# Self-attention in a decoder layer: the projection bank is copied to an on-chip tile by ScalarE, and Pool splits v from the copy

## The chip, the cores and the metric

The kernel runs on one core of one Trainium2 chip. A core has a matrix engine (TensorE; PE in the profile, PEld for its weight loads), a vector engine (VectorE, DVE), a scalar engine (ScalarE, ACT), a general one (Pool, POOL) and SyncE (SP), which issues DMA transfers. Each engine works through its own list of instructions in order; they wait for one another by semaphores. TensorE writes its products to PSUM banks; the other tiles are on-chip (SBUF). The metric is the device time of one execution in microseconds.

## The reference, cut to what matters

A decoder layer: self-attention with rotary embedding on a layer-normed x, then a cross-attention block, then a mixture of experts. The change is in the first.

```python
q, k, v = (proj(Wq), proj(Wk), proj(Wv))            # [4 batches, 16 heads, 1024, 64], fp32
q = q * cos + rotate_half(q) * sin
k = k * cos + rotate_half(k) * sin
scores = jnp.einsum('bhqd,bhkd->bhqk', q, k) / math.sqrt(HD)
scores = jnp.where(causal, -jnp.inf, scores)
attn = jax.nn.softmax(scores, axis=-1)
out = jnp.einsum('bhqk,bhkd->bhqd', attn, v)
```

## The kernel before, in words

`self_attention` runs over 4 batches and, in each, over 8 pairs of heads (`j` counts pairs over all batches). fp32 accuracy comes from splitting each operand into a high part (a copy that rounds, name `_hi`) and the rest (a subtraction, name `_lo`); so a projection is three matmuls for each 128 rows of the contraction.

**Stages.** In each batch a `prologue` norms and transposes x (`xt_hi`, `xt_lo`), and projects pair 0. Then `attention(j)` computes pair j and at the same time projects pair j + 1: its 24 steps (one for each block of 128 keys of a unit; four units, a head and 512 queries each) are taken in 8 groups of 3, and each group projects one block `t` of 128 rows of the next pair into the bank `ps_qkv`: 128 columns each of q, k and v for two heads. TensorE's part of this, `qkv` (L336 to L350), is cut into 12, 6 and 6 matmuls at places 0, 1 and 2 of the group. The last pair of a batch projects nothing. The middle six attentions are a loop of three rounds with two pairs each; the branch back is taken twice in each batch.

**The order in a step** is written out by hand for each engine. TensorE: transposes of the probabilities (L431, which at a unit's first step wait until its rows are normalised), scores ahead (L371 to L375), the values' product of the step before (L415, L416), at place 1 the transposes of the rotated q and k (L359), then the projection part (L345). At place 0 this part waits for `qkv_read`, since there is one bank.

**The bank's readers.** After the last part, ScalarE copies v's high part (`split_v`, L479). VectorE then, in `rotate`, multiplies q and k by cos (L630, `r_cos`) and sin (L633, L634, `r_sin`), subtracts v's rest (L635), which signals `qkv_read`, and adds both products (L640, `rotated`). Then it takes the reciprocals of row sums (L663), for which ScalarE's `normalise` (L500) waits.

**The weights.** Pair j + 2's weights come in 8 blocks of 128x384 through 4 slots, `w_raw`: block k uses slot k % 4. ScalarE makes `w_hi` (L470): blocks 0 and 1 at step 22 of attention j, 2 and 3 at step 23, 4 and 5 at step 0 of attention j + 1, 6 and 7 at step 1. Pool makes `w_lo` (L274) in `rest_of_w`. SyncE loads block k + 4 (L231) once `w_lo` of block k is done. TensorE waits for `w_lo` of each block at the first of its three matmuls in block t = 0 of the next projection. At steps 0 and 1 ScalarE's exponentials (L492) come behind its weight blocks in its list.

**Pool's list** in a pair: w_lo 4 to 7, the store of the pair before's last unit, three stores (L298), w_lo 0 to 3 of the pair after next. Pool can't read PSUM in this kernel and never does.

## Time and profile before

| | us |
|---|---|
| median of 3 runs (8266.21 to 8268.61) | 8266.89 |
| span of the profiled execution (first to last instruction), which is its own time here | 8265.9 |
| TensorE busy in it | 7509.6 (91%) |
| VectorE, ScalarE, Pool busy | 4437.6, 3440.3, 1747.3 |

How to read it: the profile records the start and the duration of each instruction of one execution. Busy time is the union of an engine's instructions. An idle time is put down to the engine, line and tile whose signal came last; "issue" means that nothing in the profile shows what the engine waited for. Times within a stretch are counted from the span's start. The granted clock (PEclk) is TensorE's clock as a share of 2.4 GHz.

### The profile page before, as it was taken

The page shows a single profiled execution, that of the slowest core. Times are in us where ns is not written, and L with a number is a line of the kernel's source. Part 1 is how long each engine was busy: PE and PEld are TensorE (multiplying, and loading weights), DVE is VectorE, ACT ScalarE, POOL GpSimd, SP SyncE. Part 2 cuts the span into 40 slices and gives each one's busy share as a digit, 9 for nine tenths or more (in the row PEclk, how much of TensorE's full clock was granted, in tenths as well). Part 3 has the DMA queues.
Part 4 walks back from the last instruction along what each step waited for, and adds up shares of the span by engine and source line. Part 5 has one row for each costly group of instructions (what it writes and reads, how often), then busy time and mean ns, then how long its engine had stood idle before and what let it go on. Part 6 is the DMA issues. An engine that isn't in the chain of part 4 may idle for free.

```text
span 8265.9 us, 154435 instructions
## 1 busy us (share of the span) xinstructions
PE 7509.6 (91%) x49303; PEld 6709.6 (81%) x49304; DVE 4437.6 (54%) x9784; ACT 3440.3 (42%) x7330; POOL 1747.3 (21%) x1447
## 2 busy tenths in 40 slices
PE   8988998998996899866999999999999999999999
PEld 7877877887885777756888888888888888888888
DVE  6666666666664434455555555555454554555444
ACT  5665665665663212102333333333333333333333
POOL 1111111111110000002222233222222332333222
PEclk9999999999998999978999999999999999999999
DMA  1101101101102221114555555555555555555544
GB/s 56 32 24 49 31 24 49 32 24 49 32 24 75 72 83 61 64 46 119 139 139 137 138 139 138 139 137 138 134 142 126 143 145 126 142 145 139 131 126 115
DMA packets 419950, 786.53 MB, mean 95 GB/s; under 512 B 31120, under 2 KB 295312, under 8 KB 419600
## 3 DMA queue, kind: packets, MB, share of 16 engines
q0 software_dynamic: 89328, 328.81, 18.6%
q1 hardware_dynamic: 330272, 453.35, 16.9%
q8 instruction: 184, 3.01, 0.2%
q14 instruction: 166, 1.36, 0.1%
HBM read 578.60 MB, written 203.46 MB: 95 GB/s over the span
## 4 chain that ended last, share of the span: by engine, by line
PE 38%; issue 7%; POOL 6%; ACT 3%; ACTq 1%; DVE 0%; POOLq 0%; DMA 0%; DVEq 0%
PE ps_gu L1546 8%; PE ps_gu L1548 8%; PE ps_gu L1547 8%; POOL dn_lo L1530 4%; PE ps_y L1546 4%; PE ps_y L1547 3%; PE ps_y L1548 3%; PE ps_xe L1565 2%; ACT gu_hi L1662 2%; PE ps_h L1599 1%; POOL out L1524 1%; ACT y_out L1651 1%; ACTq L1459 1%; ACT xe_hi L1640 0%; DVE at_lo L1726 0%
## 5 line engine op out<-in xcount | busy, mean ns | idle before, releaser
L1546 PE MATMUL ps_gu<-gu_hi,xe_hi 128*128 128x256 f32 x6888 | 1983.3, 288 | 62.5 <-DVE gu_lo L1794 58.2
L1548 PE MATMUL ps_gu<-gu_hi,xe_lo 128*128 128x256 f32 x6888 | 1949.6, 283 | 0.0
L1547 PE MATMUL ps_gu<-gu_lo,xe_hi 128*128 128x256 f32 x6888 | 1949.2, 283 | 0.0
L1546 PEld LDWEIGHTS ps_gu<-gu_hi,xe_hi 128*128 128x128 f32 x6888 | 1323.5, 192 | 115.1 <-DVE gu_lo L1794 85.2
L1547 PEld LDWEIGHTS ps_gu<-gu_lo,xe_hi 128*128 128x128 f32 x6888 | 1321.5, 192 | 7.8
L1548 PEld LDWEIGHTS ps_gu<-gu_hi,xe_lo 128*128 128x128 f32 x6888 | 1320.1, 192 | 0.0
L1805 DVE TENSOR_TENSOR act_h<-ps_gu,silu 128x128 f32<-128x128 f32 x861 | 248.1, 288 | 1824.9 <-ACT silu L1673 1824.9
L1673 ACT ACTIVATE silu<-ps_gu 128x128 f32<-128x128 f32 x861 | 238.9, 277 | 1685.5 <-PE ps_gu L1548 1678.8
L1546 PE MATMUL ps_y<-dn_hi,ht_hi 128*128 128x512 f32 x1722 | 724.2, 421 | 108.5 <-POOL dn_lo L1530 108.5
L345 PE MATMUL ps_qkv<-w_hi,xt_hi 128*128 128x384 f32 x1920 | 708.7, 369 | 52.0 <-DVE v L635 51.9
L1524 POOL DMA_INDIRECT out<-y_out,scatter_i x287 | 516.4, 1799 | 1011.6 <-ACT y_out L1651 974.6
L1514 POOL DMA_INDIRECT x_rows<-rows,gather_i x289 | 283.8, 982 | 2005.2 <-DVE gather_i L1756 1969.5
L1547 PE MATMUL ps_y<-dn_lo,ht_hi 128*128 128x512 f32 x1722 | 687.1, 399 | 0.0
L1548 PE MATMUL ps_y<-dn_hi,ht_lo 128*128 128x512 f32 x1722 | 686.1, 398 | 0.0
L705 DVE TENSOR_TENSOR pt_lo<-ps_t,pt_hi 128x512 fp32r<-128x512 f32 (+3 forms) x768 | 425.0, 553 | 449.7 <-ACT pt_hi L554 437.0
L1651 ACT ACTIVATE y_out<-ps_y,w_now 128x1024 f32<-128x1024 f32 x288 | 320.2, 1112 | 804.1 <-PE ps_y L1548 622.3
L345 PE MATMUL ps_qkv<-w_hi,xt_lo 128*128 128x384 f32 x1920 | 651.0, 339 | 0.0
L345 PE MATMUL ps_qkv<-w_lo,xt_hi 128*128 128x384 f32 x1920 | 648.9, 338 | 0.0
L1530 POOL TENSOR_TENSOR dn_lo<-dn_raw,dn_hi 128x512 fp32r<-128x512 f32 x256 | 520.6, 2061 | 158.7 <-ACT dn_hi L1667 158.7
L554 ACT ACTIVATE pt_hi<-ps_t 128x512 fp32r<-128x512 f32 (+3 forms) x768 | 374.5, 488 | 343.1 <-PE ps_t L431 328.8
L1546 PEld LDWEIGHTS ps_y<-dn_hi,ht_hi 128*128 128x128 f32 x1722 | 328.5, 191 | 226.7 <-POOL dn_lo L1530 163.8
L1794 DVE TENSOR_TENSOR gu_lo<-gu_raw,gu_hi 128x512 fp32r<-128x512 f32 x768 | 472.9, 683 | 2.4 <-ACT gu_hi L1662 0.2
(273 smaller groups left out, 15357.6 us busy)
## 6 DMA issues: line engine op xcount, KB each, us to landing
gu_raw<-w_gu SPq DMA_DIRECT2D x192, 1024.0 KB, 10.3
dn_raw<-w_down SPq DMA_DIRECT2D x192, 512.0 KB, 4.8
w_raw<-wqkv SPq DMA_DIRECT2D x260, 192.0 KB, 2.6
out<-residual SPq DMA_DIRECT2D x33, 512.0 KB, 2.6
probs<-x SPq DMA_DIRECT2D x32, 512.0 KB, 3.5
attn_out<-out_t POOLq DMA_DIRECT2D x128, 128.0 KB, 2.2
residual<-x SPq DMA_DIRECT2D x32, 512.0 KB, 4.4
stage<-attn_out SPq DMA_DIRECT2D x32, 512.0 KB, 5.2
```

The costliest lines, as they stand in the source:

```text
L345: mm = pe.matmul(out, xs[:, k, a], ws[:, k, :], start=(n == 0), stop=(n == 3 * HB - 1))
L554: act.activation(pt_hi[:, s % 2, off:], ps_t[:, (TB - 1 + at) % 2, off:], ACT.Copy).then_inc(tile_hi_ok, 1)
L705: dve.tensor_tensor(pt_lo[:, s % 2, off:], ps_t[:, (TB - 1 + at) % 2, off:], raw(pt_hi[:, s % 2, off:]), ALU.subtract).then_inc(tile_lo_ok, 1)
L1514: pool.indirect_dma_start(x_rows[:, :], None, rows, bass.IndirectOffsetOnAxis(ap=gather_i[:, 0:1], axis=0)).then_inc(rows_in, 16)
L1524: pool.indirect_dma_start(out, bass.IndirectOffsetOnAxis(ap=scatter_i[:, 0:1], axis=0), y_out[:, :], None, compute_op=ALU.add).then_inc(y_ ...
L1530: pool.tensor_tensor(dn_lo[:, f, a], dn_raw[:, f, a], raw(dn_hi[:, f, a]), ALU.subtract).then_inc(dn_lo_ok, 1)
L1546: pe.matmul(out, a_hi, w_hi, start=first, stop=False)
L1547: pe.matmul(out, a_hi, w_lo, start=False, stop=False)
L1548: return pe.matmul(out, a_lo, w_hi, start=False, stop=last)
L1651: act.activation(y_out[:, :], ps_y[:, :], ACT.Copy, scale=w_now[:, 0:1]).then_inc(y_ok, 1)
L1794: dve.tensor_tensor(gu_lo[:, f, a], gu_raw[:, f, a], raw(gu_hi[:, f, a]), ALU.subtract).then_inc(lo_ok, 1)
L1805: dve.tensor_tensor(act_h[:, f, :], ps_gu[:, f % 2, P:W], silu[:, f, :], ALU.mult).then_inc(h_ok, 1)
```

## The change

ScalarE no longer splits v out of the bank: it copies all 384 columns of the bank to a new on-chip tile, `qkv_sb`, and that copy signals `qkv_read`. VectorE's three products read `qkv_sb` and wait for the copy. v's two operations, the rounding copy and the subtraction, go to Pool, from `qkv_sb`. `qkv_sb` is one tile, so ScalarE's copy waits until VectorE's three products and Pool's subtraction of the block before are done. TensorE waits for v's rest before each values product. Pool's list is new: in a pair, w_lo 4 to 7 and the last store, then eight `split_v` with the three stores between (before blocks 2, 5 and 6), and only then w_lo 0 to 3 of the pair after next. Its loop now has two pairs to a round, as the other engines' has. In the prologue Pool splits v of block t - 3 after the root for block t.

```diff
+        qkv_sb = m.sb("qkv_sb", [P, W])
...
+            def split_v(j, slot, t):
+                n = j * TB + t
+                pool.wait_ge(qkv_read, START + n + 1)
+
+                pool.wait_ge(pv_ok, START + (j - 1) * NS)
+                stand_alone(pool, passed)
+                whole = qkv_sb[:, 2 * P:W].rearrange("p (h d) -> p h d", d=HD)
+                pool.tensor_copy(v[slot][:, t, :, 0, :], whole).then_inc(v_hi_ok, 1)
+                pool.wait_ge(v_hi_ok, START + n + 1)
+                pool.tensor_tensor(v[slot][:, t, :, 1, :], whole, raw(v[slot][:, t, :, 0, :]), ALU.subtract).then_inc(v_lo_ok, 1)
...
                 for t in range(1, TB):
                     find_rstd(b, t)
+                    if t >= 3:
+                        split_v_first(j, t - 3)
...
+            STORE_BEFORE = {2: 0, 5: 1, 6: 2}
+
+            def during(b, pair, j, slot, weights):
+
+                for t in range(TB):
+                    if t in STORE_BEFORE:
+                        store(b, pair, STORE_BEFORE[t])
+                    split_v(j + 1, 1 - slot, t)
+                if weights:
+                    for k in range(SLOTS):
+                        rest_of_w(j + 2, k)
...
-                for u in range(NU - 1):
-                    store(b, 0, u)
-                for k in range(SLOTS):
-                    rest_of_w(b * NP + 2, k)
-                with pool.Fori(1, NP - 1) as pair:
-                    for k in range(SLOTS, HB):
-                        rest_of_w(b * NP + pair + 1, k)
-
-                    store(b, pair - 1, NU - 1)
-                    for u in range(NU - 1):
-                        store(b, pair, u)
-                    for k in range(SLOTS):
-                        rest_of_w(b * NP + pair + 2, k)
+                    rest_of_w(j + 1, k)
+                during(b, 0, j, 0, True)
+                with pool.Fori(0, (NP - 2) // 2) as two:
+                    for i in range(2):
+                        pair = two * 2 + 1 + i
+                        for k in range(SLOTS, HB):
+                            rest_of_w(j + pair + 1, k)
+
+                        store(b, pair - 1, NU - 1)
+                        during(b, pair, j + pair, 1 - i, True)
...
                 pe.wait_ge(tile_lo_ok, START + tile)
+                pe.wait_ge(v_lo_ok, START + j * TB + kb + 1)
...
-            def split_v(j, slot, t, bank):
+            def empty_bank(j, t, bank):
                 act.wait_ge(qkv_ok, START + j * TB + t + 1)
-                act.activation(v[slot][:, t, :, 0, :], bank[:, 2 * P:W].rearrange("p (h d) -> p h d", d=HD), ACT.Copy).then_inc(v_hi_ok, 1)
+
+                act.wait_ge(rot_step, START + (j * TB + t) * 3)
+                act.wait_ge(v_lo_ok, START + j * TB + t)
+                act.activation(qkv_sb[:, :], bank[:, 0:W], ACT.Copy).then_inc(qkv_read, 1)
...
-            def rotate(j, slot, t, bank, turned):
+            def rotate(j, t, turned):
...
-                dve.wait_ge(v_hi_ok, START + n + 1)
+                dve.wait_ge(qkv_read, START + n + 1)
...
-                dve.tensor_tensor(v[slot][:, t, :, 1, :], bank[:, 2 * P:W].rearrange("p (h d) -> p h d", d=HD),
-                                  raw(v[slot][:, t, :, 0, :]), ALU.subtract).then_inc(qkv_read, 1)
                 dve.wait_ge(rot_step, START + n * 3 + 3)
```

`rotate`'s two views of `bank` become views of `qkv_sb`. `split_v_first` is `split_v` for pair 0 of a batch, with the wait for `pv_ok` that ScalarE had.

## Rows read from the trace of the kernel before

**Rows 1.** Windows: from:to, length; PE, PEld, DVE, ACT, POOL busy; PEclk, DMA, GB/s

```profile
0.00:2525.00 2525.00, 2235.72 (x13312) 1987.63 (x13313) 1642.47 (x3873) 1543.29 (x3238) 374.09 (x467) 0.96 0.13 36
155.00:225.00 70.00, 66.93 (x412) 59.89 (x412) 48.28 (x118) 47.43 (x103) 10.43 (x12) 1.00 0.12 32
```

**Rows 2.** Waits in 0:2525; columns: who waited for whom, us in total, times, longest

```profile
PE ps_qkv L345 <- DVE v L635: 51.9, 112, 0.9
...
PE ps_s L371 <- DVE qk_hi L649: 32.6, 32, 1.4
...
DVE inv_sum L663 <- issue: 28.2, 8, 4.2
...
PEld ps_qkv L345 <- POOL w_lo L274: 1.6, 5, 0.4
```

**Rows 3.** Timeline from 235 to 240 us, group 0: start, duration, instruction, [idle before]

```profile
235.48 0.28 ACT L479 ACTIVATE v<-ps_qkv 128x128 fp32r<-128x128 f32 x1 [0.28 <-PE ps_qkv L345]
...
235.88 0.42 DVE L630 TENSOR_TENSOR r_cos<-ps_qkv,cos_sb 128x256 f32<-128x256 f32 x1 [0.17 <-ACT v L479]
...
236.81 0.68 DVE L640 TENSOR_TENSOR rotated<-r_cos,r_sin 128x512 f32<-128x512 f32 x1
...
236.95 0.45 PE L345 MATMUL ps_qkv<-w_hi,xt_hi 128*128 128x384 f32 x1 [0.81 <-DVE v L635]
...
237.60 1.15 ACT L500 ACTIVATE probs<-probs,inv_sum 128x1024 f32<-128x1024 f32 x1 [0.49 <-DVE inv_sum L663]
...
239.15 0.60 PE L431 MATMUL ps_t<-ident,probs 128*128 128x128 f32 x4
```

**Rows 4.** Timeline at 217.4 us, group 6 of the pair before

```profile
217.43 0.44 PE L345 MATMUL ps_qkv<-w_hi,xt_hi 128*128 128x384 f32 x1 [0.16 <-DVE v L635]
```

**Rows 5.** Timeline from 222 to 233.4 us, the end of a pair

```profile
222.52 1.98 POOL L274 TENSOR_TENSOR w_lo<-w_raw,w_hi 128x384 fp32r<-128x384 f32 x2 [14.87 <-ACT w_hi L470]
...
224.50 0.26 ACT L479 ACTIVATE v<-ps_qkv 128x128 fp32r<-128x128 f32 x1
...
225.24 2.44 POOL L274 TENSOR_TENSOR w_lo<-w_raw,w_hi 128x384 fp32r<-128x384 f32 x2 [0.75 <-ACT w_hi L470]
...
225.73 1.08 DVE L640 TENSOR_TENSOR rotated<-r_cos,r_sin 128x512 f32<-128x512 f32 x1
...
226.20 0.39 PE L345 MATMUL ps_qkv<-w_hi,xt_hi 128*128 128x384 f32 x1
...
228.27 0.93 ACT L470 ACTIVATE w_hi<-w_raw 128x384 fp32r<-128x384 f32 x2
...
233.09 0.49 PE L371 MATMUL ps_s<-qk_hi 128*128 128x512 f32 x1 [1.12 <-DVE qk_hi L649]
```

**Rows 6.** Group by shape in 0:2525; columns: count, busy us, mean ns, idle before

```profile
L554 ACT ACTIVATE pt_hi<-ps_t 128x384 fp32r<-128x384 f32 x128 | 61.6, 481 | 3.2 <-PE ps_t L431 3.2
```

**Rows 7.** Groups by shape on Pool, whole span

```profile
L865 POOL TENSOR_SCALAR mix_rstd<-mix_mean_var 128x1 f32<-128x1 f32 x64 | 12.2, 190 | 1061.0 <-DVE mix_mean_var L1116 1061.0
...
L103 POOL TENSOR_SCALAR_AFFINE_SELECT ident<-ident 128x128 f32<-128x128 f32 x1 | 0.3, 297 | 0.2 <-POOL minus_half L99 0.2
```

**Rows 8.** The tiles w_lo and rotated; columns: count, ns least/median/most, first and last start

```profile
L274 POOL TENSOR_TENSOR w_lo<-w_raw,w_hi x260: 990/1007/1503, 13.0 to 2458.2; 128x384 fp32r<-128x384 f32 x130
...
L640 DVE TENSOR_TENSOR rotated<-r_cos,r_sin x256: 677/680/1086, 34.6 to 2457.7; 128x512 f32<-128x512 f32 x128
```

**Rows 9.** DMA issues of the page; columns: count, KB each, median us to landing

```profile
w_raw<-wqkv SPq DMA_DIRECT2D x260, 192.0 KB, 2.6
```

**Rows 10.** Busy time by stretch at two loop branches, columns as in rows 1

```profile
294.00:296.00 2.00, 0.25 (x3) 0.05 (x1) 2.00 (x6) 1.93 (x6) 1.25 (x3) 1.00 0.58 150
296.00:298.00 2.00, 1.69 (x7) 1.50 (x8) 0.37 (x1) 0.13 (x1) 1.22 (x1) 0.61 0.54 158
298.00:300.00 2.00, 2.00 (x10) 1.91 (x9) 0.38 (x2) 0.65 (x2) 0.00 (x0) 0.53 0.43 115
437.00:440.00 3.00, 2.11 (x15) 1.99 (x16) 1.81 (x5) 1.37 (x4) 2.41 (x2) 1.00 0.58 156
```

More of the change, by code:

```diff
@@ L290, in prologue, with split_v_first @@
                         rest_of_w(j, SLOTS + 2 * t - 1)
+                for t in range(TB - 3, TB):
+                    split_v_first(j, t)
                 for k in range(SLOTS):
                     rest_of_w(j + 1, k)
+            def split_v_first(j, t):
+                pool.wait_ge(pv_ok, START + j * NS)
+                n = j * TB + t
+                pool.wait_ge(qkv_read, START + n + 1)
+                stand_alone(pool, passed)
+                whole = qkv_sb[:, 2 * P:W].rearrange("p (h d) -> p h d", d=HD)
+                pool.tensor_copy(v[0][:, t, :, 0, :], whole).then_inc(v_hi_ok, 1)
+                pool.wait_ge(v_hi_ok, START + n + 1)
+                pool.tensor_tensor(v[0][:, t, :, 1, :], whole, raw(v[0][:, t, :, 0, :]), ALU.subtract).then_inc(v_lo_ok, 1)
             def store(b, pair, u):
@@ L303, in _ @@
             with pool.Fori(0, B) as b:
-                prologue(b, b * NP)
+                j = b * NP
+                prologue(b, j)
                 for k in range(SLOTS, HB):
-                    rest_of_w(b * NP + 1, k)
-                for u in range(NU - 1):
-                    store(b, 0, u)
-                for k in range(SLOTS):
-                    rest_of_w(b * NP + 2, k)
-                with pool.Fori(1, NP - 1) as pair:
-                    for k in range(SLOTS, HB):
-                        rest_of_w(b * NP + pair + 1, k)
-                    store(b, pair - 1, NU - 1)
-                    for u in range(NU - 1):
-                        store(b, pair, u)
-                    for k in range(SLOTS):
-                        rest_of_w(b * NP + pair + 2, k)
+                    rest_of_w(j + 1, k)
[7 more added lines that the diff above has]
+                        during(b, pair, j + pair, 1 - i, True)
                 store(b, NP - 2, NU - 1)
@@ L520, in prologue @@
                 act.wait_ge(s_ok, START + j * NQ)
-                act.wait_ge(pv_ok, START + j * NS)
                 for i in range(ROUNDS):
@@ L530, in prologue @@
                     if 0 <= t < TB:
-                        split_v(j, 0, t, ps_qkv if t % 2 else ps_o)
+                        empty_bank(j, t, ps_qkv if t % 2 else ps_o)
                     for n in FIRST_SCORES.get(i, ()):
@@ L562, in attention @@
                     if place == PER - 1 and not last:
-                        if group == 0:
-                            act.wait_ge(pv_ok, START + j * NS)
-                        split_v(j + 1, 1 - slot, group, ps_qkv)
+                        empty_bank(j + 1, group, ps_qkv)
                     if place == 1 and group == 0:
@@ L618, in rest_of_x @@
                                   raw(xt_hi[:, :, t * P:(t + 1) * P]), ALU.subtract).then_inc(xt_lo_ok, 1)
-            def rotate(j, slot, t, bank, turned):
+            def rotate(j, t, turned):
                 n = j * TB + t
-                dve.wait_ge(v_hi_ok, START + n + 1)
+                dve.wait_ge(qkv_read, START + n + 1)
                 half_d = HD // 2
-                qk = bank[:, 0:2 * P].rearrange("p (a h d) -> p a h d", a=2, d=HD)
+                qk = qkv_sb[:, 0:2 * P].rearrange("p (a h d) -> p a h d", a=2, d=HD)
                 s = r_sin[:, :, :].rearrange("p (a h) d -> p a h d", a=2)
@@ L630, in rotate @@
                 dve.tensor_tensor(r_cos[:, :, :].rearrange("p (a h) (c d) -> p a (h c) d", a=2, c=2),
-                                  bank[:, 0:2 * P].rearrange("p (a h d) -> p a h d", a=2, d=half_d),
+                                  qkv_sb[:, 0:2 * P].rearrange("p (a h d) -> p a h d", a=2, d=half_d),
                                   cos_sb[:, t, :, :].unsqueeze(2).broadcast_to([P, 2, 4, half_d]), ALU.mult).then_inc(rot_step, 1)
@@ L684, in prologue @@
                     if t >= 0:
-                        rotate(j, 0, t, ps_qkv if t % 2 else ps_o, j * NT + t)
+                        rotate(j, t, j * NT + t)
                     for n in FIRST_SCORES.get(i, ()):
@@ L714, in attention @@
                     if place == PER - 1 and not last:
-                        rotate(j + 1, 1 - slot, group, ps_qkv, first_tile(j) + tiles["qk", group] + 1)
+                        rotate(j + 1, group, first_tile(j) + tiles["qk", group] + 1)
                     if place == 1 and group == 0:
```

2 lines of the change are left out of this document (1 added, 1 removed).

## The prediction

> **What bounds the kernel now.** The change touches self-attention alone, so I first asked which stretch that is and how full TensorE is in it. The windows [rows 1] give it: attention is the first 2525 us of 8266, and TensorE is busy in 2236 of them; in one pair of heads (155 to 225 us) it is busy 66.9 of 70 us, with VectorE at 48, ScalarE at 47 and Pool at 10. TensorE bounds this stage, so what counts is each place where it stands still. The list of waits [rows 2] names them. The one that the change is about is `PE ps_qkv L345 <- DVE v L635`: 51.9 us in 112 waits, four in each of the 28 pairs that project a next pair (7 in each of 4 batches), 1.86 us a pair. The second, `PE ps_s L371 <- DVE qk_hi L649`, 32 times, about 1 us, is early in every pair. The third, `DVE inv_sum L663 <- issue`, 8 times, 28.2 us in all, is VectorE at the branch of the loop over two pairs, twice in each batch: there it waits for nothing that the profile shows. Pool's w_lo stops TensorE's loads for 1.6 us in all: its work is in time today.
>
> The timeline around one bank wait [rows 3] shows what goes on: the last projection ends at 235.4, ScalarE takes v (0.28), VectorE does four reads of the bank, TensorE goes on at 236.95 after 0.81 us of idleness. The reader should also see what comes behind: VectorE's rotated (236.81), the reciprocal, ScalarE's normalise until 238.75, and TensorE's transposes of these rows at 239.15. The timeline at a pair's end [rows 5] shows the other chain: ScalarE splits weight blocks, Pool makes w_lo 0 and 1 from 222.52 to 224.50, w_lo 2 and 3 from 225.24 to 227.68, TensorE wants the first of them at 226.20.
>
> **The bank is free earlier.** ScalarE's copy of 384 columns out of PSUM costs what pt_hi of 128x384 costs, 0.48 us [rows 6], in place of 0.28. The bank is free 0.5 us after the projection instead of 1.36, so 0.84 us earlier; the largest wait is 0.81, and all 112 go. That is not yet time. The four of a pair are 0.81 (group 0 [rows 3]), 0.16 twice (groups 2 and 6, one of them in [rows 4]), and what is left of 1.86, some 0.72, in group 4. After those of 0.16 nothing is due soon: 0.16 x 56 = 9 us gained. After those of groups 0 and 4 (56 in all), the next step transposes rows that ScalarE has normalised only 0.4 us before (238.75 against 239.15 [rows 3]). If VectorE's chain keeps its time, TensorE gains 0.4 us and not 0.8. The chain starts later by 0.14 (copy until 235.96, so r_cos at 236.0) and loses v's 0.2, so it keeps its time: 0.4 x 56 = 22 us gained, if Pool doesn't disturb it.
>
> **Pool disturbs it.** Now VectorE's three products and Pool's copy and subtraction start on the same signal, all out of on-chip memory. What two such engines do to each other is in [rows 5, 8]: rotated takes 0.68 us mostly, but 1.08 at 225.73, where the w_lo that Pool began at 225.24 ran until 226.25; and these two w_lo take 2.44 together, where the two before took 1.98. Each engine waited for the other to end. Pool's price: a one-input pass over 128x128 took 0.30 us, a one-column operation 0.19 [rows 7], w_lo of 384 columns 1.01 [rows 8]; so 0.19 + (1.01 - 0.19)/3 = 0.46 for the subtraction (bounds 0.34, a third of w_lo, and 1.01, all of it) and 0.30 for the copy. In turns: r_cos 236.0 to 236.34, copy to 236.64, r_sin to 236.84, subtraction to 237.3, r_sin to 237.5; rotated starts 0.69 late, the normalise ends at 239.44, and TensorE is 0.3 us later than before. So groups 0 and 4 lie between -0.4 and +0.3 us each; I take +0.1, nearer the contended row: +6 us (bounds -22, +17). The other groups have room: their normalised rows are not wanted in the next step.
>
> The Trainium skill says the same of the port (SBUF — State Buffer, "Who interferes with whom"): a VectorE instruction with two SBUF inputs contends with a GpSimd instruction that reads SBUF, and the loser blocks fully. It speaks against this change, since before only rotated had both inputs there; the trace agrees, by the 1.08 us at 225.73. By the rule the 0.3 us would hold at all 56 places, 17 us and not 6.
>
> **The pair's end, the costly step.** In `during`, `rest_of_w(j + 2)` of blocks 0 to 3 comes after all eight `split_v`, and the eighth waits for the eighth bank. Before, blocks 0 and 1 were ready at 224.50, before that bank was even read. Now, with the times of [rows 5]: copy 224.50 to 224.98; r_cos, Pool's copy, r_sin, subtraction, r_sin in turns to 226.5; w_lo 0 to 227.5; rotated's 0.6 between; w_lo 1 to 229.1, w_lo 2 to 230.1, w_lo 3 to 231.1. TensorE, at its place at 226.20, waits for each block; its part ends at 231.65 instead of 228.4 (twelve matmuls take 2.2, as from 236.95 to 239.15): 3.3 us late. Behind w_lo stands SyncE: block 5 is loaded into block 1's slot, 2.6 us after w_lo 1 [rows 9], at 231.7, and ScalarE splits blocks 4 and 5 in front of its exponentials: it ends at 232.2 instead of 229.20, and exponentials, normalise, qk_hi, VectorE's qk_hi and the wait at 233.09 move by 3.0 us. TensorE's own lateness is absorbed in that wait down to 2.2, so ScalarE's 3.0 sets the end. Bounds: if Pool is never held, w_lo 1 is done at 227.6 and the delay is 1.5; if its two new operations cost 1.0 each, 4.2.
>
> A stall of this size can also cost clock. At a loop's branch TensorE was busy for 0.25 of 2 us, and the granted clock was then 0.61 and 0.53 over the next two stretches; at the other branch of this batch, with TensorE busy 2.1 of 3 us, it stayed at 1.00 [rows 10]. Those two stretches lost 2 x 0.39 + 2 x 0.47 = 1.7 us of full clock (the lower level is 1.2 GHz, half of the upper), of which the wait at 233.09 hides some 0.7; that is 1.0 more. The waits here are cut up by matmuls, so I count it at half the places: 0.5.
>
> How often: weights for pair j + 2 matter at the ends of attention 0 to 5, 24 in all. In 8 of them the engines wait at the loop's branch anyway (VectorE for 28.2 / 8 = 3.5 us [rows 2]), which hides nearly all: 0.5 each, 4 us (bounds 0 and, should Pool's longer loop body be fetched anew as TensorE's is, 3 each). The other 16: 3.5 x 16 = 56 us (bounds 24 and 83, the latter with the clock at every place).
>
> The rest is small. Prologue: empty_bank waits for the turn before, long done; VectorE sheds 0.2 us a round, of which few lie on the path: -1 us (bounds -3, +3). The stores move past one or two split_v, with half a pair until their buffer is wanted. TensorE's extra wait per weigh step is met long before, and matmuls are queued ahead of it: 0.
>
> **Sum.** 56 + 4 + 6 - 9 - 1 = +56 us on the execution of span 8265.9: 8322. The runs' median is 1 us above that span: 8323.
>
> **Rivals.**
> 1. Half of it: VectorE and Pool don't meet (Pool's requests fall into gaps, or it starts behind). Then groups 0 and 4 give 22, 2 and 6 give 9, and the pair's ends cost 1.9 (w_lo 1 at 228.0) x 16 = 30, plus 2: about 8267, no difference. For it: only one rotated in a pair is seen held now. Against: each new pair of operations starts on one signal. 0.18.
> 2. The other side, faster: w_lo is wanted later than I reckon, so that Pool's place in the queue costs little and the freed bank decides: -31 for the waits and under 1 us x 16: 8236 to 8250. It decides below 1 us a pair's end. Against: TensorE wants w_lo 0 at 226.20 and w_lo 3 (227.68 now) within 0.2 us of its making. 0.07.
> 3. Worse: the clock falls at every pair's end (+8), Pool's body is fetched anew at the branch (+20), Pool's operations cost 1.0 rather than 0.4 (+19): 8340 to 8375. For it: VectorE pays 3.5 us at the branch. Against: Pool runs 12 operations in a pair [rows 1] and 28 after, against VectorE's 118. 0.23.
>
> The Trainium skill (Runtime: NRT & Kernel Launch, "Instruction fetch mechanics") says a taken branch whose target is outside the two pages held stalls the engine for a fetch; the waits called issue fit that, and nothing here shows Pool's side, whose body grows. That would make rival 3.
>
> **How the numbers follow.** Forecast 0.52, at 8323 (own range 8295 to 8345), rivals 0.18, 0.07 and 0.23. What a measurement here can tell from no change is 0.2%, 16.5 us. Slower by more: forecast and rival 3, 0.75; within: 0.18; faster: 0.07. The range takes in rival 1 and nearly all of rival 3: 8264 to 8368.
>
> **What would show it.** The waits on DVE v L635 are gone and the bank's wait is nearly nil. TensorE waits for POOL w_lo by some 40 to 60 us where it was 1.6, and ScalarE's w_hi for the DMA by as much. Four of the seven steps from pair to pair in a batch take 3 us more, and the growth lies in the first two steps of the pair that begins. VectorE's products show 0.3 to 0.5 us more than 0.28 and 0.42 wherever Pool runs. I am wrong if w_lo 0 ends within 1.5 us of the last projection, if the normalise before group 0's transposes doesn't move (then 20 us less), or if 8 pair's ends with the branch cost as much as the others (then 20 us more).

## The result, and the profile after

The kernel after takes 8295.4 us (median of 7 runs, 8287.4 to 8304.7) against 8266.9 for the kernel before (7 runs beside them): ratio 1.0033, 95% interval 1.0022 to 1.0044. It is slower, by 28.5 us and not by the 56 that I forecast. The profiled run of after is the slowest of its seven, 8304.7 us with a span of 8303.1, which is 37.2 us above the span of before; the comparison below is of these two executions, so some 9 us of that difference are this execution's distance from its median.

First the list of waits of the kernel after, over attention (window 0:2560; who waited for whom, us in all, times, longest):

```profile
ACT w_hi L507 <- DMA w_raw<-wqkv: 87.4, 52, 8.8
PE ps_t L468 <- ACT probs L540: 81.8, 72, 3.4
PEld ps_qkv L381 <- POOL w_lo L275: 66.1, 94, 1.6
PE ps_qkv L381 <- POOL w_lo L275: 40.1, 87, 1.5
...
PE ps_s L407 <- DVE qk_hi L683: 30.8, 32, 1.4
DVE inv_sum L697 <- issue: 20.5, 8, 2.7
...
PEld ps_qkv L381 <- ACT qkv_sb L519: 12.9, 55, 0.2
```

The wait for `v` of [rows 2] is gone; what is left for the bank is the last row, weight loads that wait at most 0.2 us for ScalarE's copy. In its place TensorE waits for Pool's w_lo, 66.1 us before its weight loads (1.6 in [rows 2]) and 40.1 before its matmuls, and ScalarE's w_hi for its load, 87.4 us in 52 waits. TensorE's transposes wait for normalised rows in 72 places, 56 more than before; the wait for qk_hi is hardly changed from the 32.6 of [rows 2]. The wait for loads in the same view of before:

```profile
ACT w_hi L470 <- DMA w_raw<-wqkv: 42.7, 14, 8.4
```

The timeline of after at the pair's end that [rows 5] show of before; here the last projection ends at 227.17:

```profile
227.34 0.49 ACT L519 ACTIVATE qkv_sb<-ps_qkv 128x384 f32<-128x384 f32 x1
...
228.03 0.42 POOL L284 CAST v<-qkv_sb 128x128 fp32r<-128x128 f32 x1 [6.92 <-ACT qkv_sb L519]
228.21 0.38 DVE L669 TENSOR_TENSOR r_sin<-qkv_sb,sin_sb 128x128 f32<-128x128 f32 x1
...
228.53 0.58 POOL L286 TENSOR_TENSOR v<-qkv_sb,v 128x128 fp32r<-128x128 f32 x1
...
228.82 0.83 DVE L674 TENSOR_TENSOR rotated<-r_cos,r_sin 128x512 f32<-128x512 f32 x1
229.07 4.35 POOL L275 TENSOR_TENSOR w_lo<-w_raw,w_hi 128x384 fp32r<-128x384 f32 x4
...
230.57 0.45 PE L381 MATMUL ps_qkv<-w_hi,xt_hi 128*128 128x384 f32 x1 [1.48 <-POOL w_lo L275]
...
233.08 0.53 ACT L507 ACTIVATE w_hi<-w_raw 128x384 fp32r<-128x384 f32 x1 [1.82 <-DMA w_raw<-wqkv]
...
235.11 0.52 ACT L507 ACTIVATE w_hi<-w_raw 128x384 fp32r<-128x384 f32 x1 [1.51 <-DMA w_raw<-wqkv]
235.66 0.90 ACT L532 ACTIVATE probs<-ps_s,neg_max 128x768 f32<-128x768 f32 x1
```

Pool turns to the four w_lo at 229.07, behind the split of v. TensorE stands for the first, ScalarE waits for two loads, which had waited for w_lo's slots, and its exponentials start at 235.66. Windows of the same stretch (length; PE, PEld, DVE, ACT, POOL busy; PEclk) show what this does to the clock:

```profile
226.00:229.40 3.40, 3.04 (x21) 2.58 (x19) 2.69 (x7) 3.19 (x10) 1.29 (x3) 1.00 0.00 0
229.40:232.80 3.40, 1.97 (x7) 1.24 (x8) 2.59 (x5) 1.83 (x4) 3.40 (x4) 0.90 0.24 66
232.80:236.00 3.20, 3.20 (x13) 2.89 (x12) 0.00 (x0) 1.39 (x3) 1.90 (x3) 0.58 0.67 181
```

In the second window TensorE was busy 1.97 of 3.40 us. From 232.1 on the granted clock was 0.50, the lower of its two levels, for 3.4 us. Of the 16 ends without a loop's branch this came behind 7; at the other 9 the clock stayed at 1.00 until the next block's last projection.

The durations (tile views: ns least, median, most) show Pool and VectorE meeting. In attention (x224) Pool's two operations are longer than in the prologue (x32), where VectorE is elsewhere, and VectorE's two are longer in the median than their least, 281 and 691 ns:

```profile
L284 POOL CAST v<-qkv_sb x224: 405/416/507, 97.8 to 2488.6; 128x128 fp32r<-128x128 f32 x112
L286 POOL TENSOR_TENSOR v<-qkv_sb,v x224: 579/585/595, 98.4 to 2489.1; 128x128 fp32r<-128x128 f32 x112
L317 POOL CAST v<-qkv_sb x32: 291/292/527, 34.5 to 1976.4; 128x128 fp32r<-128x128 f32 x32
L319 POOL TENSOR_TENSOR v<-qkv_sb,v x32: 457/464/829, 35.1 to 1976.8; 128x128 fp32r<-128x128 f32 x32
```

```profile
L669 DVE TENSOR_TENSOR r_sin<-qkv_sb,sin_sb x256: 281/378/383, 34.8 to 2488.8; 128x128 f32<-128x128 f32 x128
...
L674 DVE TENSOR_TENSOR rotated<-r_cos,r_sin x256: 691/835/843, 35.5 to 2489.4; 128x512 f32<-128x512 f32 x128
```

**Where the time went.** To place it I read from both traces when the last projection of each block ends (256 of them), and took the growth of the difference from one to the next. A pair is eight such steps; "behind block t" is the step that starts with the release of block t's bank. There are 28 pairs with such steps, 16 pair's ends without a loop's branch ("16 ends" in the table) and 8 with one ("8 ends"). The rest is the starts of the batches and of their second pairs. Values in us, against the profiled execution of before; the experiments are in the same table, since all of what follows is read from it.

```
kernel                      behind block (each, x56; 3: x28)   8 ends  16 ends      rest  attention
                             0, 4   1, 5   2, 6     3    sum   branch  each    sum          in all
after                        0.24  -0.16  -0.44  0.00  -20.2    -5.9   2.97   51.8    5.6     31.4
e1_weights_before_last_v     0.24  -0.16  -0.44  0.00  -20.2     3.0   1.39   22.3    4.9      9.9
e2_order_alone               0.00   0.00   0.01  0.00    0.5    -5.5   2.35   38.6    3.6     37.2
e3_pool_after_rotated        0.00  -0.16  -0.44  0.00  -33.4     5.7   1.39   22.3    6.6      1.2
e4_early_bank_alone          0.09  -0.16  -0.44  0.00  -28.6    -1.5   0.78   13.6   10.4     -6.0
e5_free_waits_first         -0.14  -0.16  -0.44  0.00  -41.6     2.6   1.25   20.1    7.0    -11.9
e6_bank_held_longer          0.21   0.20   0.20  0.15   37.9    -8.9   0.00    0.0    8.7     37.7
e7_last_block_from_bank      0.00  -0.16  -0.44  0.00  -33.4    -5.2   0.35    5.7    5.4    -27.5
e8_both                     -0.14  -0.16  -0.44  0.00  -41.5    -6.6   0.20    3.3    2.7    -42.2
e9_after_free_waits_first    0.09  -0.16  -0.44  0.00  -28.2    -7.7   2.72   45.1    1.0     10.1
e10_after_last_from_bank     0.24  -0.16  -0.44  0.00  -20.2    -6.6   2.59   43.8    5.8     22.8
e12_pool_at_once             0.09  -0.16  -0.44  0.00  -28.4    -2.0   0.21    4.3    5.7    -20.3
e13_copy_v_only_last        -0.14  -0.16  -0.44  0.00  -41.6    -4.3   0.00    1.1   -1.0    -45.7
```

("Each" of the 16 ends is their median; their mean in the kernel after is 3.24. Behind the 9 ends without a drop of the clock the median is 2.83, and the 7 with one have 3.67 in the mean. In e9 the 11 ends at full clock have 2.69, in e10 the 15 such ends 2.59.) The steps behind blocks repeat to a few hundredths from pair to pair and from run to run. The ends with a branch and the rest do not: they differ by up to 15 and 11 us between the kernels, also where nothing in them was changed (e6), so single profiles say little of a few us there. Two things can be seen all the same. One of the 8 ends is 1.6 to 3.4 us shorter in twelve of the thirteen kernels than in the kernel before, so that much of each sum is most likely a long stop of before's own execution. And the three kernels e1, e3 and e5 have +2.6 to +5.7 where e7, e8, e12 and e13 have -2.0 to -6.6; what sets these two groups apart comes out below.

So the 31.4 us of attention are 51.8 at sixteen pair's ends, less 20.2 inside the pairs, less 0.3 in all the rest. My sum had 56 and -3.

### The profile page after: what moved, and what is told of

Its sections match the earlier page's. It is cut to its first block, busy times and chain, and to the rows that moved or that the text cites. A ratio compares the mean times of both kernels' runs of the same rounds, so it can differ in the third digit from the quotient of the medians.

```text
span 8303.1 us, 156335 instructions
## 1 busy us (share of the span) xinstructions
PE 7532.2 (91%) x49302; PEld 6723.7 (81%) x49304; DVE 4467.3 (54%) x9528; ACT 3496.4 (42%) x7330; POOL 1989.2 (24%) x1959
## 4 chain that ended last, share of the span: by engine, by line
PE 38%; issue 6%; POOL 5%; ACT 3%; ACTq 1%; DVE 1%; DVEq 0%; POOLq 0%; DMA 0%
PE ps_gu L1580 8%; PE ps_gu L1582 8%; PE ps_gu L1581 8%; POOL dn_lo L1564 4%; PE ps_y L1580 4%; PE ps_y L1582 3%; PE ps_y L1581 3%; PE ps_xe L1599 2%; ACT gu_hi L1696 2%; PE ps_h L1633 1%; POOL out L1558 1%; ACT y_out L1685 1%; ACTq L1493 0%; ACT xe_hi L1674 0%; DVE at_lo L1760 0%
## 5 line engine op out<-in xcount | busy, mean ns | idle before, releaser
L381 PE MATMUL ps_qkv<-w_hi,xt_hi 128*128 128x384 f32 x1920 | 705.7, 368 | 41.8 <-POOL w_lo L275 40.1
L468 PE MATMUL ps_t<-ident,probs 128*128 128x128 f32 x2304 | 403.2, 286 | 90.0 <-ACT probs L540 81.8
```

The source lines that it names most:

```text
L381: mm = pe.matmul(out, xs[:, k, a], ws[:, k, :], start=(n == 0), stop=(n == 3 * HB - 1))
L468: mm = pe.transpose(ps_t[:, (TB - 1 + at) % 2, i * P:(i + 1) * P], probs[g][:, i, kb * P:(kb + 1) * P], ident[:, :])
```

## The experiments

Each was timed in 5 rounds beside the kernel before; ratios are to it, with the 95% interval.

### The two suspects taken apart: the place of w_lo in Pool's queue, and Pool beside VectorE

**e1_weights_before_last_v**: the kernel after, `during` with the weights one place sooner, in front of the eighth split.

```diff
                 for t in range(TB):
                     if t in STORE_BEFORE:
                         store(b, pair, STORE_BEFORE[t])
+                    if weights and t == TB - 1:
+                        for k in range(SLOTS):
+                            rest_of_w(j + 2, k)
                     split_v(j + 1, 1 - slot, t)
-                if weights:
-                    for k in range(SLOTS):
-                        rest_of_w(j + 2, k)
```

> The changed kernel, with one move in Pool's list: w_lo 0 to 3 of the pair after next stand before the eighth split_v and not behind it. My theory (the growth is the pair's end, where w_lo comes late): the 16 pair's ends that cost 3.2 us each in the changed kernel's trace (51.8 us in all) cost 0 to 0.5, TensorE's wait for w_lo falls from 40 us to under 8, ScalarE's wait for the weights' load (87 us) to what it was before (43), and what is left is the gain inside the pairs, 0.71 us in each of 28, some 20 us, less what the batches' starts lost (5): 8240 to 8258. Rival A (Pool's reads hold VectorE up and that is the loss): the time stays near 8295, since as many operations of Pool meet VectorE's. Rival B (Pool's longer list as such): 8280 to 8295.

Measured: 8281.81 us, ratio 1.0016 (1.0007 to 1.0025), 14 us less than the kernel after. That is not my 8240 to 8258, and lies in the range that I gave to rival B, Pool's longer list as such. The traces tell the two apart. ScalarE's wait for loads is back where it was, and TensorE's weight loads wait for w_lo 5.9 us, from the list of waits of this kernel:

```profile
ACT w_hi L507 <- DMA w_raw<-wqkv: 42.1, 14, 8.5
...
PEld ps_qkv L381 <- POOL w_lo L275: 5.9, 16, 0.4
```

The order of w_lo thus costs 1.85 us at each of the 16 ends in the mean (3.24 to 1.39, 29.5 in all): 1.44 by the ends at full clock (2.83 to 1.39), the rest where the clock fell, which it does behind none of the 16 ends here. But 1.39 stays, to within 0.02 at every end, where I had expected next to nothing: something else lies at the pair's end. Of the 29.5 us, 8.9 don't show in attention's sum, since the 8 ends with a branch are longer by that.

**e2_order_alone**: the kernel before, in which Pool waits for the eighth bank before w_lo 0 to 3, so that it has the lateness without any of the new work.

```diff
+                    pool.wait_ge(qkv_read, START + (b * NP + pair + 2) * TB)
                     for k in range(SLOTS):
                         rest_of_w(b * NP + pair + 2, k)
```

> The kernel before, with one wait added on Pool: w_lo 0 to 3 of the pair after next wait until the eighth bank is read. Nothing else of the change. My theory: w_lo 0 then ends 1.36 + 0.1 + 1.0 = 2.5 us after the last projection (3.2 in the changed kernel), so each of the 16 pair's ends without a branch costs 2.3 to 2.8 us, and the 8 with a branch little: 8267 + 37 to 45 = 8304 to 8312, slower than the changed kernel itself, since here nothing is gained inside the pairs. Rival A (contention is the loss): under 10 us, 8267 to 8277.

Measured: 8305.23 us, ratio 1.0043 (1.0029 to 1.0058), as expected. The order alone costs 2.35 us at an end and 38.6 in all, without a gain inside the pairs to set against it, and this kernel is no faster than the kernel after (the intervals overlap).

**e3_pool_after_rotated**: e1, in which Pool's split of v also waits for VectorE's rotation of the block.

```diff
                 pool.wait_ge(qkv_read, START + n + 1)
+                pool.wait_ge(rot_ok, START + n + 1)
```

> As the kernel with w_lo before the last split_v, and in attention each split_v waits until VectorE has written rotated, so that Pool's two operations never run beside the three products. My theory of the contention: r_sin falls back from 0.38 to 0.28 and rotated from 0.83 to 0.68, the normalise in front of group 0's and 4's transposes ends 0.35 us sooner, and 56 places gain that: 20 us less than the kernel that differs by this wait alone. Rival A (the order of w_lo was all, VectorE has room): no difference between the two beyond 3 us. Rival B (Pool's operations, now later, meet VectorE or w_lo elsewhere): slower by up to 10 us.

Measured: 8272.24 us, ratio 1.0006 (0.9996 to 1.0015); 10 us less than e1 (8 by the ratios), half of what I expected. The step behind blocks 0 and 4 goes from 0.24 to 0.00, 13 us in 56 places, and rotated is 692 ns in the median (680 before). Two things fell short. The pair's end stayed at 1.39. And without Pool in the way these steps are at 0.00 and not below it, for which the traces have the reason. In medians over the 56 places, r_cos starts 0.75 us after the last projection where it started 0.39 after it before: the copy starts 0.15 later and takes 0.21 longer. The subtraction of v, now Pool's, gives back only 0.07. So the normalise ends 3.56 us after the last projection instead of 3.27, and the transposes behind it, which used to start 0.40 after its end, now start 0.05 after it: 3.62 against 3.67.

**e4_early_bank_alone**: the kernel before, but ScalarE copies the whole bank first and then v's high part from the copy; VectorE's four operations read the copy, and Pool does what it did before.

```diff
-                act.activation(v[slot][:, t, :, 0, :], bank[:, 2 * P:W]..., ACT.Copy).then_inc(v_hi_ok, 1)
+                act.wait_ge(rot_step, START + (j * TB + t) * 3)
+                act.wait_ge(v_lo_ok, START + j * TB + t)
+                act.activation(qkv_sb[:, :], bank[:, 0:W], ACT.Copy).then_inc(qkv_read, 1)
+                act.wait_ge(qkv_read, START + j * TB + t + 1)
+                act.activation(v[slot][:, t, :, 0, :], qkv_sb[:, 2 * P:W]..., ACT.Copy).then_inc(v_hi_ok, 1)
```

> The early bank without Pool: ScalarE copies the whole bank and then takes v's high part from the copy, VectorE reads the copy for its four operations, Pool's list is that of the kernel before. My theory: all waits for the bank go, inside a pair groups 1, 2, 5 and 6 gain 0.15, 0.44, 0.15 and 0.43 us as in the changed kernel's trace, and groups 0 and 4, whose chain to the normalise is not held by Pool, gain another 0.2 to 0.6 each where the changed kernel lost 0.25 and 0.21 there: 1.5 to 2.3 us a pair, 42 to 64 us: 8203 to 8225. Rival (ScalarE's list, longer by 0.2 and 0.28 us a group, becomes the bound in groups 0 and 4 and at a pair's start): a gain of under 1.2 us a pair, 8235 to 8255.

Measured: 8260.56 us, ratio 0.9991 (0.9982 to 1.0). It misses both expectations: the early release gains 33 us behind blocks 1, 2, 5 and 6 and loses 5 behind 0 and 4 and some 14 at the pair's ends, though Pool has none of the new work. The 33 us are the same as in every kernel with the early copy. The pair's end lost 0.78 with the order of before. Its trace says by what: at the 16 ends rotated starts 0.37 us later after the last projection than in the kernel before (1.65 against 1.28), and as it then meets w_lo 2 nearer to w_lo's start it takes 1.50 us instead of 1.08. No run of its own tests this.

### What the remaining 1.39 us at a pair's end are

The timeline of e3 at a pair's end answers; the last projection ends at 153.9:

```profile
154.03 0.49 ACT L520 ACTIVATE qkv_sb<-ps_qkv 128x384 f32<-128x384 f32 x1
...
155.01 2.06 POOL L275 TENSOR_TENSOR w_lo<-w_raw,w_hi 128x384 fp32r<-128x384 f32 x2 [1.10 <-ACT w_hi L508]
155.10 1.10 DVE L671 TENSOR_TENSOR r_sin<-qkv_sb,sin_sb 128x128 f32<-128x128 f32 x1
...
156.23 1.39 DVE L675 TENSOR_TENSOR rotated<-r_cos,r_sin 128x512 f32<-128x512 f32 x1
157.54 0.15 DVE L698 RECIPROCAL inv_sum<-row_sum 128x1 f32<-128x1 f32 x1
...
157.72 0.83 ACT L541 ACTIVATE probs<-probs,inv_sum 128x640 f32<-128x640 f32 x1 [1.12 <-DVE inv_sum L698]
...
158.58 0.60 ACT L549 ACTIVATE out_t<-ps_o 64x512 f32<-64x512 f32 x1
```

Pool's w_lo 2 and 3 run beside the rotation, as they did before. But r_sin now has both inputs on chip, like rotated: it takes 1.10 instead of 0.28 and ends 0.15 us after the w_lo that began at 155.01; rotated then meets the next w_lo and takes 1.39 (1.09 before). The reciprocal comes 3.69 us after the last projection where it came 2.30 after it, later by the same 1.39 as the pair's end. The same stretch of the kernel before, last projection at 154.9, has:

```profile
154.91 0.26 ACT L479 ACTIVATE v<-ps_qkv 128x128 fp32r<-128x128 f32 x1
...
155.66 2.44 POOL L274 TENSOR_TENSOR w_lo<-w_raw,w_hi 128x384 fp32r<-128x384 f32 x2 [0.75 <-ACT w_hi L470]
155.74 0.28 DVE L634 TENSOR_TENSOR r_sin<-ps_qkv,sin_sb 128x128 f32<-128x128 f32 x1
...
157.15 0.15 DVE L663 RECIPROCAL inv_sum<-row_sum 128x1 f32<-128x1 f32 x1
```

A second difference stands in the first lines: the copy starts 0.17 us after the last projection here, 0.05 before. In `empty_bank` two waits that were satisfied long ago stand behind the one for the projection. The next four kernels test both and, in e6, how to read TensorE's waits.

**e7_last_block_from_bank**: e3, with the eighth block rotated from the bank; every other block from the copy as before.

```diff
-                        rotate(j + 1, group, first_tile(j) + tiles["qk", group] + 1)
+                        rotate(j + 1, group, first_tile(j) + tiles["qk", group] + 1,
+                               ps_qkv if group == TB - 1 else qkv_sb)      # r_cos, r_sin read this
...
                             pe.wait_ge(qkv_read, START + j * TB + TB + group)
+                            if group == 0:
+                                pe.wait_ge(rot_step, START + (j * TB + TB) * 3)
```

> The kernel that splits v after the rotation and w_lo before the last v, with one edit: the eighth block of a pair is rotated by VectorE from the projection bank (after ScalarE's copy of it, as ever), not from the on-chip tile; TensorE's first group of the next pair waits for those reads. Theory: the +1.39 us that each pair's end still has is VectorE held by Pool's w_lo 2 and 3, above all in the second r_sin (1.10 against 0.28), since both its inputs lie in the on-chip memory now; with one input in the bank it is 0.28 again, the reciprocal comes about 0.8 to 1.1 us sooner, and each of 16 to 24 pair's ends gives 0.8 to 1.1 us back: span 8242 to 8254, against 8268.8. Rival 1: the hold only moves, to the addition of the two products (both on chip in every kernel), which then takes 1.8 instead of 1.4: 0.4 to 0.5 us each, span 8257 to 8262. Rival 2: the pair's end is set by something else (w_raw's loads): within 2 us of 8268.8.

Measured: 8238.87 us, ratio 0.9970 (0.9958 to 0.9982), span 8237.3, 5 us below my range. The pair's end is at 0.35 instead of 1.39 in all sixteen, and r_sin takes 280 ns there again. The theory holds, and neither rival: 1.04 us at an end was VectorE held by w_lo, 0.82 of it in r_sin and 0.22 in rotated, which takes 1.17 instead of 1.39. The 8 ends with a branch fell too, by 10.9 us in all; that, and the two groups of kernels named under the table (3.8 us against -4.5 in the mean, 8.3 apart, 8 x 1.04), say that the hold was paid at these ends as well. They scatter too much for a single pair of profiles to show it.

**e5_free_waits_first**: e3, with the two satisfied waits ahead of the one that ends last. **e8_both**: this and e7's edit.

```diff
-                act.wait_ge(qkv_ok, START + j * TB + t + 1)
                 act.wait_ge(rot_step, START + (j * TB + t) * 3)
                 act.wait_ge(v_lo_ok, START + j * TB + t)
+                act.wait_ge(qkv_ok, START + j * TB + t + 1)
```

> The kernel of the run before with its eight-block order kept, and one edit: ScalarE's two waits of the whole-bank copy that are long satisfied (rotation's steps, v's low part) stand ahead of the wait for the projection, not behind it. In the kernel after, the copy begins 0.17 to 0.19 us after the last projection, in the kernel before 0.04. If the waits behind the one that ends last cost that, the copy begins at about 0.04 and each of the 24 pair's ends and each of groups 1 to 3 and 5 to 7 gains up to 0.15 us at most (in groups 1 to 3 and 5 to 7 only where TensorE is held by the bank): span 8258 to 8266, against 8268.8 with the waits behind. Rival: the start is not due to the number of waits but to the copy being on another path (its input is ready no sooner): copy still at 0.17 and span within 1.5 us of 8268.8.

> Both edits together: the last block rotated from the bank, and the satisfied waits ahead of the projection's. If the two are independent, their gains add: span 8235 to 8250, time at 0.996 to 0.998 of the kernel before. If the copy's later start is not on the path, equal to the run with the last block from the bank alone within 2 us.

Measured: e5 8260.09 us, 0.9994 (0.9985 to 1.0003); e8 8217.89 us, 0.9945 (0.9931 to 0.9959), 47 us faster than the kernel before. In e8 the copy starts 0.05 us after the last projection:

```profile
154.97 0.47 ACT L521 ACTIVATE qkv_sb<-ps_qkv 128x384 f32<-128x384 f32 x1
...
155.48 0.42 DVE L667 TENSOR_TENSOR r_cos<-ps_qkv,cos_sb 128x256 f32<-128x256 f32 x1
...
155.94 2.43 POOL L275 TENSOR_TENSOR w_lo<-w_raw,w_hi 128x384 fp32r<-128x384 f32 x2 [0.96 <-ACT w_hi L510]
156.02 0.28 DVE L671 TENSOR_TENSOR r_sin<-ps_qkv,sin_sb 128x128 f32<-128x128 f32 x1
...
157.41 0.15 DVE L698 RECIPROCAL inv_sum<-row_sum 128x1 f32<-128x1 f32 x1
```

Moving two waits that never wait gave 0.14 us behind blocks 0 and 4 and 0.14 at each pair's end, with either kernel around it: 8 us and some 3 in the table. The ratios say more, 10 us from e3 to e5 and 21 from e7 to e8, and the spans of both came out below my ranges (8254.1 and 8211.6, against 8258 to 8266 and 8235 to 8250). 12 of e8's 54 us of span lie behind attention, where nothing was changed; what the runs' medians have beyond the table I can't place.

**e6_bank_held_longer**: the kernel before with one more subtraction of v, its result unused, in front of the one that releases the bank.

```diff
+                dve.tensor_tensor(spare[:, :, :], bank[:, 2 * P:W]..., raw(v[slot][:, t, :, 0, :]), ALU.subtract)
                 dve.tensor_tensor(v[slot][:, t, :, 1, :], bank[:, 2 * P:W]..., raw(v[slot][:, t, :, 0, :]),
                                   ALU.subtract).then_inc(qkv_read, 1)
```

> The kernel before, with one more VectorE subtraction of v in front of the one that releases the projection bank (0.25 us by the row of that subtraction), its result not used. Theory: what the bank's hold costs is the wait seen by TensorE's weight loads (106 us in 168 waits, six groups of every pair), since the end of a matmul in the trace is modelled and swallows half of the idle time. Then the added time lands in six groups of 28 pairs, 168 times 0.25 = 42 us, and the rest of the chain (groups 0 and 4, pair's end) adds at most 0.25 x 80 = 20: span 8305 to 8335. Rival, my prediction's reading: only the 112 groups of the matmul rows are held by the bank (112 x 0.25 = 28): increments of about 0.25 in four of eight groups and none in the other two; span 8290 to 8300.

Measured: 8306.27 us, ratio 1.0052 (1.0038 to 1.0066), 42 us above before. The profiled span, 8300.2, lies under my 8305 to 8335, at the edge of the rival's 8290 to 8300, so the span doesn't decide; the steps do. All seven steps of a pair grew, six by 0.2 and the one behind block 3 by 0.15, and the pair's ends not at all. The bank's waits of this kernel:

```profile
PEld ps_qkv L346 <- DVE v L638: 139.0, 168, 1.2
...
PE ps_qkv L346 <- DVE v L638: 73.9, 112, 1.0
```

and the one row of the kernel before that [rows 2] lack:

```profile
PEld ps_qkv L345 <- DVE v L635: 106.0, 168, 1.1
```

The weight loads' wait grew by 33 us, 168 times 0.2, and the steps inside the pairs by 37.9; the matmuls' wait grew by 22. Six steps of a pair grew and not four: the reading from weight loads holds, but for the step behind block 3, which it hadn't either (a true lateness of 0.15 shows there as 0.09). Mine, from the matmuls, doesn't.

### The same edits on the kernel after, and how far it goes

**e9_after_free_waits_first**: the kernel after with e5's edit. **e10_after_last_from_bank**: the kernel after with e7's edit, the order of w_lo left as it is. The diffs are those above.

> The kernel after, with one edit: the two long satisfied waits of ScalarE's whole-bank copy stand ahead of the wait for the projection. If the 0.14 us that this gave with the other edits in place is independent of them, it is worth 0.14 us in 56 groups (first and fifth of 28 pairs) and in 24 pair's ends, 8 + 3 = 11 us: time 8282 to 8287 where the kernel after has 8295. If w_lo's lateness hides it at the pair's end, 8 us alone; the rival, that it is worth nothing here, gives 8293 to 8298.

> The kernel after, with one edit: the eighth block is rotated from the projection bank. In the kernel after, Pool makes w_lo only after it has split the eighth v, so VectorE's products are not held by w_lo there, and TensorE is late for w_lo in every case. If that reading is right, this edit alone is worth less than 0.3 us at a pair's end (0.1 us by which r_sin was held by the split of v): time 8288 to 8297. If instead the VectorE chain sets the pair's end in the kernel after too, it is worth 1 us in 16 to 24 places: 8270 to 8280.

Measured: e9 8278.35 us, 1.0017 (1.0008 to 1.0026), by the ratios 13 us below the kernel after; the table places 8 behind blocks 0 and 4 and 7 at the ends. Of these 7 the edit itself explains 2, by the ends at full clock 0.14 each (2.83 to 2.69); the rest is the clock and two single long ends of the kernel after. e10 8293.21 us, 1.0033 (1.0022 to 1.0043): the same as the kernel after, within its range, with 0.4 us less at an end by the medians and 0.24 by the ends at full clock, as against my 0.3 at most. So the edit that is worth 1.04 us at an end when w_lo is in time is worth 0.24 there when it isn't: in the kernel after w_lo's place in the queue is the binding one, and w_lo comes too late to hold r_sin. The end of w_lo 0 shows it (medians after the last projection): 3.34 us in after, 3.21 in e9, 3.10 in e10, where VectorE no longer holds Pool's split, and 2.82 in e2, and the ends at full clock follow with 2.83, 2.69, 2.59 and 2.33.

**e12_pool_at_once**: e8 with e3's wait taken out again. **e13_copy_v_only_last**: e8, ScalarE copying of the eighth bank only v.

```diff
-                act.activation(qkv_sb[:, :], bank[:, 0:W], ACT.Copy).then_inc(qkv_read, 1)
+                act.activation(qkv_sb[:, c:W], bank[:, c:W], ACT.Copy).then_inc(qkv_read, 1)   # c = 2 * P for block 7
```

> The fastest kernel so far, with Pool's split of v allowed again while VectorE rotates. By the first pair of runs that differed in this (inside the pairs -20 and -33 us), Pool's split in the way of r_sin and rotated costs 0.24 us in the first and fifth group of 28 pairs, 13 us: ratio 0.9955 to 0.9965 where it had 0.9945, pair's ends unchanged at +0.20.

> The fastest kernel so far, with ScalarE copying only the v columns of the eighth block's bank (VectorE reads q and k of that block from the bank). The copy of 128 columns took 0.26 us in the kernel before, that of 384 takes 0.47: each of 24 pair's ends is 0.20 us shorter and stands at 0.00 against the kernel before, 3 to 5 us in all: time 8212 to 8216 where it had 8217.9. The rival, that something else holds the pair's end at +0.20, gives no change.

Measured: e12 8244.35 us, 0.9974 (0.9964 to 0.9984), 24 us more than e8 by the ratios, where I expected 13; the table shows 0.23 us more behind blocks 0 and 4 (13 us) and the rest in the places that differ from run to run, so the size stays half explained. e13 8221.03 us, 0.9944 (0.9931 to 0.9958): the pair's end is at 0.00 as forecast, but the time is e8's and not my 8212 to 8216; 2 to 3 us are below what 5 rounds tell. These two are the fastest versions: 0.55% under the kernel before.

## Why the prediction was right in sign and wrong in size

**What held.** Slower, because Pool's w_lo now stands behind the eighth split of v: e2 alone makes it so, e1 takes it away. The forecast for a pair's end was 3.5 us; measured 3.24 in the mean, 51.8 us for 56. Both parts of it held: 3.0 for the delay against 2.83 at the ends at full clock, and for the clock 1.0 at half of the ends against 0.84 at 7 of 16. The way it goes held too: TensorE's matmuls wait 40.1 us for w_lo (forecast 40 to 60), ScalarE's wait for loads is up by 45, and w_lo 0 ends 3.34 us after the last projection (forecast 227.5 against 224.45, so 3.05).

**Right in kind, too small.** The start of groups 0 and 4 is a loss, as I took it: 0.24 us each against my 0.1 (+13 us against +6). There the Trainium skill's rule (SBUF — State Buffer, "Who interferes with whom") was nearer than my choice: the 0.3 at all 56 places that I worked out by it against 0.24 measured, and 0.00 when Pool starts after rotated (e3). That the engines take turns is borne out by all meetings of these operations in attention (last section). That 0.3 came so near is in part luck: I had rotated start 0.69 us late, with Pool's subtraction in front of the second r_sin. The subtraction waits for Pool's copy and came behind that r_sin, so rotated started 0.38 late and was then itself held by 0.14.

**The step that failed** is "After those of 0.16 nothing is due soon: 0.16 x 56 = 9 us gained." That term was mis-sized. Measured (the sums of these steps): 24.6 us behind blocks 2 and 6, 0.44 each, and 8.7 behind blocks 1 and 5, 0.16 each, where I had seen no wait at all: 33 us in place of 9. Of the 27.5 us by which the forecast (56) missed the medians (28.5), these are 24. The same 33 us are in all eleven kernels with the early copy, whatever else is changed, and e6 shows the reading that finds them. At 217.43 [rows 4] the matmul row says 0.16 idle. But a matmul's row lasts longer than the distance at which the next can start: the matmul before it and the two behind start at 216.87, 217.70 and 217.88, so two starts are 0.56 us apart over the wait and 0.18 to 0.27 behind it. The weight-load rows of this place in the kernel before show it:

```profile
216.63 0.19 PEld L416 LDWEIGHTS ps_o<-pt_lo,v 128*128 128x128 f32 x1
217.42 0.19 PEld L345 LDWEIGHTS ps_qkv<-w_hi,xt_hi 128*128 128x128 f32 x1 [0.60 <-DVE v L635]
```

Idle for 0.60 as a weight load, and 0.16 of that is there when nothing is late (the step gained 0.44). Behind blocks 1 and 5 the loads wait 0.32 us in the mean and the matmuls not visibly; the step gained 0.16. In both, the true lateness is the load's wait less about 0.16.

**The other terms.** "8 ends with a branch: +4" came out at -5.9, but this sum moves between -8.9 and +5.7 over thirteen kernels, so the +4 is not shown; against e6, where nothing is changed at these ends (-8.9), it would be +3.0. Prologue and batch starts, forecast -1, are 5.6 in this run and between -1.0 and +10.4 in the others; also open. The count closes: the 31.4 us up to attention's last projection and 5.9 behind it, where nothing was changed, make the 37.2 of the spans; some 9 of these are this run's distance from its median.

**Missed as a mechanism, but not in the sum.** I let the chain of VectorE keep its time, because r_cos would start only 0.14 later and v's 0.2 fall away. It starts 0.36 later, and v's part gives back 0.07 (e3), so of the 0.4 us that groups 0 and 4 were to gain without Pool nothing came. 0.15 of the 0.36 are two satisfied waits behind the last one, in front of the copy (e5, e8, e9). A slip without effect: I called 0.81 the largest wait, while [rows 2] say 0.9; all 112 went. And I charged the port's price to Pool's new operations alone. Its old ones have it too, since the products now read on-chip memory: w_lo against r_sin and rotated is 1.04 us at a pair's end, the largest single price of VectorE's new source (e7). In the kernel after it isn't paid, since w_lo comes too late to meet r_sin. Taken in the order of the experiments, the 3.24 us of a pair's end are 1.85 for the order and the clock behind it (e1), 1.04 for VectorE against w_lo (e7), 0.15 for the waits (e8) and 0.20 for the longer copy (e13), down to 0.00 in the median; in another order the shares are others, as e10 shows.

Rival 1, in which the engines don't meet, is refuted by the durations of both; rival 2 by TensorE's 40.1 us; rival 3's longer stall at the branch didn't come (`DVE inv_sum L697 <- issue` 20.5 us, 28.2 before), and its Pool operations of 1.0 us were 0.42 and 0.58.

## What to carry to other kernels

Read what a late operand costs TensorE from the weight loads' rows, or from start to start, and by group: the matmul rows had 52 us of idle time where the weight loads had 106 (some 0.16 of each of these is no lateness), and nothing at all at 56 places that cost 0.16 us each. Freeing a buffer early was right, worth 33 to 42 us here; it lost because work was put in one engine's queue in front of weights due soon, and because inputs moved on chip let that engine hold the other. When sources move from the bank to on-chip memory, list what the sharing engine already does at that moment, not only what is added, and leave the one block where they meet on its old source. Put the wait that ends last at the end of the list.

## What the runs showed of the hardware that I had not expected

- Pool and an operation of VectorE with both inputs on chip took strict turns, and short operations of Pool did so as well as long ones. Where Pool's was running first, r_sin ended 0.14 to 0.16 us after Pool's and rotated 0.54 to 0.57 after it, whether Pool's was its split of v (228 meetings each in after) or a w_lo (28 each in e3, and for rotated in before). Where VectorE's was first, Pool's copy ended 0.15 us after r_cos, and w_lo 0.85 to 0.89 after r_sin or rotated. So the price goes by how much of the other's operation is left: r_sin 0.28 to 0.38 behind Pool's copy and to 1.10 behind w_lo, rotated 0.69 to 0.83 and to 1.39, while Pool's copy and subtraction go from 0.29 to 0.42 and from 0.46 to 0.58.
- With one input in the bank, r_sin beside the same w_lo took 0.28 us (before, e7, e8). Undisturbed, it takes 0.28 from the bank and 0.28 from the copy: for VectorE, where the input lies made no difference of its own.
- Two waits that are already satisfied, placed behind the one that ends, delayed the instruction by 0.12 to 0.15 us; in front of it they cost nothing that shows.
- A bank held 0.2 us longer moved seven of the eight steps of a pair by 0.15 to 0.2 us each and the pair's end by 0.00.
